# Neighbourhood attention and expert layer on one core: projections issued as late as their readers allow, a reordered opening, key loads in ScalarE's queue, image 1 loaded in pieces

## The chip, the cores and the metric

The kernel runs on one core of one Trainium2 chip. The time is the device time of one execution in microseconds. The kernel before takes 632.2 us (median of three runs, 630.95 to 632.5). The profile is of one further execution that took 633.32 us, of which 631.4 us are the recorded span.

## The reference

Two images of 48 x 48 pixels with 384 channels go through two blocks. What is computed, shortened:

```python
x = x + attention(_gn(x), registers, qkv_w, qkv_b, out_w, out_b)
x = x + experts(_gn(x), router_w, router_b, fc1_w, fc1_b, fc2_w, fc2_b)

# attention: 12 heads of 32; 16 register tokens give extra keys and values
q, k, v = split(x @ qkv_w.T + qkv_b)
k_cat, v_cat = concat(k, reg_k), concat(v, reg_v)
scores = where(mask_7x7_neighbourhood_or_register, q @ k_cat.T / sqrt(32), -1e30)
o = softmax(scores) @ v_cat
return o @ out_w.T + out_b

# experts: 4 experts with 96 hidden units each, the best 2 of a softmax router
hmid = gelu(x @ fc1.T + fc1_b) * combine
return hmid @ fc2.T + combine @ fc2_b
```

`_gn` is a group norm of 32 groups over a whole image, without weights.

## The kernel before

**Tiling.** An image has 2304 pixels: 6 tiles of 8 columns (384 pixels each, in the code `SN`) or, across them, 6 strips of 8 rows. The 12 heads are worked on in three groups of four. Image times head group makes 6 stages, and stage times tile makes 36 steps, `g` = 0 to 35. Every step has three parts, p = 0, 1, 2. Matrix products of float32 quality are made from two float16 halves: value = high + low, three products out of four.

**Units.** A unit is one projection of 384 pixels: "k" for a strip of keys (9 matmuls of 384 columns), "q" for a tile of queries (9 of the same), "v" for a tile of values (27 of 128 columns). A stage needs 18 units. TensorE computes a unit into a bank of PSUM (bank 6 in the step loop), ScalarE takes the high half out, VectorE the low half (for keys it also copies the windows into KT, `keys_low`), and a DMA writes it to DRAM: keys by SyncE (kscr), queries and values by GpSimd (qscr, vscr). They come back in another layout: KB by `keys_in` (3 DMAs a step), QS by `queries_in` (3), VR by `values_in` (6), all issued by SyncE in the kernel before. Step g's part of these is loaded one to three steps ahead.

**A part of a step.** On TensorE: scores of keys for two strips (`key_scores`, L1309), one unit of the NEXT stage (L1177), a third of the output projection of step g-2 (L1177, OS and WO), the weighted sums for two strips (`weighted`, L1328 and L1331, which need ScalarE's exponentials L984), and two groups of scores of step g+2 for the maximum (`scores`, L1279), which VectorE reduces (L609). In part 0 the maxima of step g+1 are turned (L1294), ScalarE copies them (L973) in part 1, and GpSimd sends them into two rows of QS (L413, `maxima_in`); the key scores of step g+1 wait for that DMA.

**What sets the order.** Everything is written out by hand, per engine, and bound by semaphores. In the kernel before all 18 units of stage 0 are made in the opening (six keys, then `FIRST`), and all 18 of stage n+1 within stage n by the table `NEXT`: keys in its steps 0 and 1, queries and values in steps 2 to 5. Stage 5 (steps 30 to 35) has no units; there the weighted sums lag one strip pair behind and the router's logits (L1349, L1350) stand on TensorE. The second half of the kernel, the expert layer, starts at about 484.5 us and is not touched.

**Image 1.** Its pixels are loaded by GpSimd in step 0 (L461, six DMAs of 576 KB) for the statistics and the norm; the normalised halves overwrite them in steps 6 to 11 (L914, L920, L377), and the pixels are loaded again in step 12 (L466, six DMAs of 576 KB) as the residual.

**The opening.** After the statistics of image 0, per strip: VectorE makes two float32 values (L549), ScalarE the third (L929), ScalarE three high halves (L904), VectorE three low halves (L559), then TensorE the keys of the strip.

## Time and profile before

| | |
|---|---|
| median of three runs | 632.2 us |
| profiled execution, its span | 633.32 us, 631.4 us |
| TensorE busy | 557.0 us, 88% |
| VectorE, ScalarE, GpSimd busy | 435.6, 312.5, 301.4 us |
| first key scores of step 0 (start of the step loop) | 72.40 us |
| end of step 35's last normalisation | 486.8 us |

The busy share of TensorE is high on the whole. What a change of order can win is in the stretches in which it is lower, so the windows and the chain of waits say more than the share. A step is measured below from one turn of the maxima (L1294) to the next: the turn at 75.39 us belongs to step 0, that at 91.69 us to step 1, that at 207.20 us to step 11, at 219.98 us to step 12, at 238.55 us to step 13, at 272.16 us to step 16 and at 419.10 us to step 29.

### The profile page before, as it was taken

How to read it: one execution, taken by the hardware profiler on the slowest of the kernel's cores; microseconds unless marked ns; L12 is line 12 of the kernel's file. 1: busy time of each engine (PE TensorE's matmuls, PEld its weight loads, DVE VectorE, ACT ScalarE, POOL GpSimd, SP SyncE). 2: the span in 40 equal slices, each digit the busy share in tenths (PEclk: the TensorE clock that was granted, in tenths of full speed). 3: DMA queues.
4: the chain of work that ended last, by engine and by line, in shares of the span. 5: the costliest groups of instructions: out<-in, count | busy, mean ns of one | idle time of the engine just before them, and what ended most of it. 6: DMA issues, size and time to landing. Idle time of an engine off the chain costs nothing.

```text
span 631.4 us, 22435 instructions
## 1 busy us (share of the span) xinstructions
PE 557.0 (88%) x9227; PEld 390.8 (62%) x9227; DVE 435.6 (69%) x1071; ACT 312.5 (49%) x622; POOL 301.4 (48%) x442
## 2 busy tenths in 40 slices
PE   3567969999999869999999999996988589998996
PEld 2344746767677646777677767774665346664553
DVE  6784559887976658678977898668795558763332
ACT  1762534447767624444444444556664438744321
POOL 4105746885387712556579713465554232313221
PEclk8697989999999979999999999999899799999999
DMA  9858979566866598756876588666520011211122
GB/s 309 194 140 218 277 238 219 172 174 156 198 182 167 164 320 202 206 152 182 203 186 184 156 205 210 161 175 193 128 61 6 2 38 38 77 41 54 57 76 75
DMA packets 130988, 97.79 MB, mean 155 GB/s; under 512 B 66684, under 2 KB 123944, under 8 KB 130888
## 3 DMA queue, kind: packets, MB, share of 16 engines
q1 hardware_dynamic: 120456, 73.84, 44.6%
q0 software_dynamic: 10432, 22.52, 11.5%
q8 instruction: 73, 1.20, 0.8%
q14 instruction: 27, 0.22, 0.1%
HBM read 59.83 MB, written 35.68 MB: 151 GB/s over the span
## 4 chain that ended last, share of the span: by engine, by line
PE 62%; DVE 17%; DMA 6%; issue 5%; POOL 4%; ACT 3%; SPq 2%; DVEq 0%; POOLq 0%; ACTq 0%
PE ps L1177 41%; PE ps L1309 5%; PE ps L1328 5%; PE ps L1331 4%; PE ps L1279 3%; DMA QS<-MT 3%; DVE MX L609 2%; DVE ST L511 2%; DVE KU L579 1%; DVE XH L603 1%; DMA X<-in_x 1%; DVE GT_ L549 1%; DVE KT L588 1%; PE ps L1294 1%; PE ps L1450 1%
## 5 line engine op out<-in xcount | busy, mean ns | idle before, releaser
L984 ACT ACTIVATE PT<-ps 128x448 f32<-128x448 f32 (+1 forms) x207 | 96.2, 508 | 99.0 <-PE ps L1309 98.8
L609 DVE TENSOR_REDUCE MX<-ps 128x2 f32<-128x372 f32 x216 | 106.8, 535 | 14.0 <-PE ps L1279 13.9
L1177 PE MATMUL ps<-X,WQ 128*128 128x384 f16 x486 | 89.8, 333 | 2.5 <-POOL X L377 1.6
L491 POOL TENSOR_TENSOR KT<-QS,KT 128x384 f16<-128x384 f32 x36 | 34.3, 961 | 94.6 <-ACT KT L1094 94.6
L1328 PE MATMUL ps<-PT,VR 128*32 128x112 f32 (+1 forms) x1656 | 76.6, 259 | 0.0
L1177 PE MATMUL ps<-OS,WO 128*128 128x384 f16 x324 | 70.2, 327 | 5.9 <-POOL OS L419 3.7
L1331 PE MATMUL ps<-PT,SELW 128*32 128x112 f32 (+1 forms) x1656 | 74.0, 253 | 0.0
L1177 PE MATMUL ps<-XH,WQ 128*128 128x384 f16 x324 | 62.4, 342 | 8.6 <-DVE XH L559 7.9
L1309 PE MATMUL ps<-QS,KB 122*128 122x112 f16 (+1 forms) x864 | 59.4, 213 | 11.5 <-DMA QS<-MT 11.2
L1177 PEld LDWEIGHTS ps<-X,WQ 128*128 128x128 f16 x486 | 46.1, 100 | 30.8 <-issue 4.3
L1279 PE MATMUL ps<-KB,QS 120*32 120x186 f16 x1728 | 56.8, 246 | 8.5 <-DMA QS<-qscr 5.2
L392 POOL DMA_DIRECT2D qscr<-QT x36 | 27.4, 761 | 73.4 <-DVE QT L594 70.9
L413 POOL DMA_DIRECT2D QS<-MT x72 | 37.7, 529 | 50.0 <-ACT MT L973 49.3
L1177 PE MATMUL ps<-KT,WQ 128*128 128x384 f16 x324 | 58.6, 326 | 2.9 <-DVE X L805 1.8
L1309 PEld LDWEIGHTS ps<-QS,KB 122*128 122x128 f16 x864 | 42.9, 100 | 26.4 <-issue 21.8
L1328 PEld LDWEIGHTS ps<-PT,VR 128*32 128x32 f32 x1656 | 38.8, 109 | 32.9 <-issue 29.0
L603 DVE SCALAR_TENSOR_TENSOR X<-ps,X 128x384 f32<-128x384 f32 x54 | 30.1, 557 | 39.2 <-PE ps L1177 38.7
L377 POOL TENSOR_TENSOR X<-GT_,X 128x384 f16<-128x384 f32 x36 | 35.0, 974 | 36.7 <-DVE GT_ L549 18.0
L798 DVE TENSOR_TENSOR QS<-ps,QS 128x384 f32<-128x384 f32 x36 | 19.7, 555 | 43.9 <-POOL KT L491 15.0
L1177 PEld LDWEIGHTS ps<-XH,WQ 128*128 128x128 f16 x324 | 30.8, 101 | 30.7 <-ACT XH L904 8.0
L419 POOL TENSOR_TENSOR OS<-ON,OS 128x384 f16<-128x384 f32 x36 | 32.9, 914 | 34.8 <-ACT OS L991 34.6
L1279 PEld LDWEIGHTS ps<-KB,QS 120*32 120x32 f16 x1728 | 39.3, 97 | 12.9 <-issue 7.6
(182 smaller groups left out, 1068.3 us busy)
## 6 DMA issues: line engine op xcount, KB each, us to landing
KB<-kscr SPq DMA_DIRECT2D x108, 192.0 KB, 3.8
kscr<-KT SPq DMA_DIRECT2D x36, 384.0 KB, 5.1
VR<-vscr SPq DMA_DIRECT2D x216, 56.0 KB
QS<-qscr SPq DMA_DIRECT2D x108, 96.0 KB, 3.9
...
```

What stands on the lines that cost most here:

```text
L377: nc.gpsimd.tensor_tensor(xh_block(n, blk, 1, k), tmp_block(n, k), xh_block(n, blk, 0, k), ALU.subtract).then_inc(s_["gn_lo_p"], 1)
L413: pool.dma_start(QS[SROWS + part:SROWS + part + 1, :, s * SN:(s + 1) * SN], MT[part * HEADS:(part + 1) * HEADS, g % 2, :]).then_inc(m_in[g ...
L419: nc.gpsimd.tensor_tensor(OS[:, 1, s * SN:(s + 1) * SN], ON[:, g % 2, :], OS[:, 0, s * SN:(s + 1) * SN], ALU.subtract).then_inc(s_["os_lo" ...
L491: nc.gpsimd.tensor_tensor(HW[:, m % 2, 1, k, :], HF[:, unit % 2, :], HW[:, m % 2, 0, k, :], ALU.subtract).then_inc(s_["hl"], 1)
L603: V.scalar_tensor_tensor(out=xj, in0=ps[:, op_bank(g, j), 0:SN], scalar=1 / WS, in1=xj, op0=ALU.mult, op1=ALU.add).then_inc(s_["op_done"], 1)
L609: V.tensor_reduce(out=MX[:, g % 2, t, 2 * pair:2 * pair + 2], in_=ps[:, S_BANK(i), 0:2 * RUN].rearrange("p (h n) -> p h n", h=2), op=ALU.m ...
L984: A(PTS[pt_slot(n)][:, 0:w], ps[:, ST_BANK(n), 0:w], ACT.Exp, scale=SCORE).then_inc(s_["exd"], 1)
L1177: last = mm(bank, lhsT(a, k), rhs(b, k), start=(k == 0 and n == 0), stop=(finish and k == steps - 1 and n == 2))
L1279: last = mm(ps[32 * j:32 * j + 32, S_BANK(i), hh * RUN:(hh + 1) * RUN], QS[0:SROWS, h, q0:q0 + 32], KB[0:SROWS, h, g % 4, at:at + RUN], st ...
L1309: last = mm(ps[:, ST_BANK(n), h * w:(h + 1) * w], KB[0:TROWS, h, g % 4, LEAD + CHUNK * a:LEAD + CHUNK * (a + 1)], QS[0:TROWS, h, s * SN + ...
L1328: mm(ps[DH * h:DH * (h + 1), O_BANK(g), CT_ * q0:CT_ * q1], VR[:, g % 2, a, DH * h:DH * (h + 1)], PTS[pt_slot(n)][:, h * w:(h + 1) * w], s ...
L1331: last = mm(ps[DH * h:DH * (h + 1), O_BANK(g), at:at + w], SELW[:, DH - 1 - a:2 * DH - 1 - a], PTS[pt_slot(n)][:, h * w:(h + 1) * w], star ...
```

## The change

- **Units late.** `NEXT` is replaced by `fillers(g, p)`: step g makes the values of step g+3 in part 0, the queries of step g+4 in part 1 and one key strip of the next stage in part 2, the strip (s+3) mod 6. So there are three units a step up to step 26, with one exception: the keys of stage 3 (image 1's first) are all made in steps 12 to 14, two a step, and so steps 9 to 11 have two units and steps 12 to 14 four. Steps 27 to 31 have two, step 32 one, the last three none. The lag of the weighted sums (`LAG`) begins at step 32, not 30; the router's logits and the loads and splits of the expert weights move to steps 33 and 34.
- **Opening.** 16 units instead of 18. VectorE makes all three values of a strip and the low half of the third channel block, GpSimd the low halves of the other two (`POOL_K`). The split of the first weights moves ahead of the group norm's parameters. The products of the registers and of the value bias move ahead of the first scores.
- **Key loads.** `keys_in` for steps 3 and later is issued in ScalarE's queue, between the two exponentials of part 1; in steps 3, 9, 15, 21 and 27 it first waits there until all keys of the next stage are in DRAM.
- **Image 1.** The six loads of step 0 go to steps 0 to 2, one in parts 1 and 2 each; the six of step 12 go to steps 15 to 17 in the same way.

```diff
+LAG = 32
+def fillers(g, p):
+    gi, s = divmod(g, TILES)
+    out = []
+    if p == 0:
+        out.append((gi + (s + 3) // TILES, "v", (s + 3) % TILES))
+        if gi == 2 and s < 3:
+            out.append((3, "k", 2 * s))
+    if p == 1:
+        out.append((gi + (s + 4) // TILES, "q", (s + 4) % TILES))
+    if p == 2 and gi == 2 and s < 3:
+        out.append((3, "k", 2 * s + 1))
+    elif p == 2 and (gi, s) not in ((1, 3), (1, 4), (1, 5)):
+        out.append((gi + 1 + (s + 3) // TILES, "k", (s + 3) % TILES))
+    return [u for u in out if u[0] < STAGES]
+FIRST = tuple((0, "k", i) for i in range(STRIPS)) + ((0, "q", 0), (0, "q", 1), (0, "v", 0), (0, "q", 2), (0, "v", 1), (0, "q", 3))
+BESIDE = ((0, "v", 2), (1, "k", 0), (1, "k", 1), (1, "k", 2))
-POOL_K = ((), (0, 1, 2), (0, 1, 2), ())
+POOL_K = ((0, 1), (0, 1, 2), (0, 1, 2), ())
...
 # GpSimd
-                    if g == 0:
-                        for half in range(2):
-                            at = half * 3 * SN
-                            pool.dma_start(raw1(p, at, 3 * SN), x[1, :, p, at:at + 3 * SN]).then_inc(x_in[1][p][half], 16)
-                    if g == 2 * TILES:
-                        pool.wait_ge(s_["v_mm"], 6 * KC)
...
+                    if g < KC and p:
+                        at = (p - 1) * 3 * SN
+                        pool.dma_start(raw1(g, at, 3 * SN), x[1, :, g, at:at + 3 * SN]).then_inc(x_in[1][g][p - 1], 16)
+                    if 15 <= g < 18 and p:
+                        i = 2 * (g - 15) + p - 1
...
 # VectorE, opening
             for a in range(STRIPS):
-                for k in range(2):
+                for k in range(KC):
                     normalised(0, a, k)
-                for k in range(KC):
-                    low_half(0, a, k)
+                low_half(0, a, 2)
...
 # ScalarE
+            def keys_in(g):
+                gi, s = divmod(g, TILES)
+                if s == 0:
+                    for i in range(3):
+                        act.wait_ge(kw_out[i], 32 * gi + 32)
+                if g >= 4:
+                    act.wait_ge(s_["st_mm"], 6 * (g - 3))
+                for j, part in enumerate((0, 1, 0)):
+                    nc.scalar.dma_start(KB[DH * j:DH * (j + 1), :, g % 4, LEAD:LEAD + STRIPS * CHUNK],
...
                     exps(6 * g + 2 * p)
+                    if p == 1 and g + 3 < LAST:
+                        keys_in(g + 3)
                     if gi == STAGES - 1:
                         normalised(2, s, p)
                     exps(6 * g + 2 * p + 1)
...
 # TensorE, opening
-            for a in range(STRIPS):
-                keys(0, a)
-            for kind, i in FIRST[0:6]:
-                unit(0, kind, i)
+            for u in FIRST:
+                unit(*u)
+            for g in (1, 2):
+                registers(g, 2 - g)
+            pe.wait_ge(*evicted(0, "q", 1))
+            value_bias()
             pe.wait_ge(s_["pads"], 4)
             pe.wait_ge(s_["i_in"], 16)
+            pe.wait_ge(s_["obx"], 1)
+            for p in range(3):
+                scores(0, 2 * p)
+                scores(0, 2 * p + 1)
+                unit(*BESIDE[p])
+            scores(1, 0)
+            scores(1, 1)
+            maxima_turned(0)
+            unit(*BESIDE[3])
+            for i in range(2, 6):
+                scores(1, i)
...
 # TensorE, steps
-                    if gi < STAGES - 1:
-                        unit(gi + 1, *NEXT[s][p])
+                    for u in fillers(g, p):
+                        unit(*u)
```

On TensorE the opening stood like this, from the six key strips and two query units (x72) on; x54 and x27 are value units, x9 a query unit, L1279 the scores, L1294 the turn of the maxima, the rows with RG and BVH the registers and the value bias:

```order
L1177 MATMUL ps<-XH,WQ 128x384 x72
L1177 MATMUL ps<-WQ,XH 128x128 x54
L1177 MATMUL ps<-XH,WQ 128x384 x9
L1177 MATMUL ps<-WQ,XH 128x128 x27
L1279 MATMUL ps<-KB,QS 32x186 x16
L1177 MATMUL ps<-XH,WQ 128x384 x9
L1279 MATMUL ps<-KB,QS 32x186 x16
L1177 MATMUL ps<-WQ,XH 128x128 x27
L1279 MATMUL ps<-KB,QS 32x186 x16
L1177 MATMUL ps<-XH,WQ 128x384 x9
```

And in the changed kernel, from the last query unit ahead of the registers to the first key scores of the loop (L1203 are the projections, L1311 the scores, L1324 the turn, L1339 the key scores):

```order
L1203 MATMUL ps<-RG,WQ 128x16 x9
L1203 MATMUL ps<-WQ,RG 16x128 x9
L1203 MATMUL ps<-BVH,WO 128x1 x27
L1311 MATMUL ps<-KB,QS 32x186 x16
L1203 MATMUL ps<-WQ,XH 128x128 x27
L1311 MATMUL ps<-KB,QS 32x186 x16
L1203 MATMUL ps<-XH,WQ 128x384 x9
L1311 MATMUL ps<-KB,QS 32x186 x16
L1203 MATMUL ps<-XH,WQ 128x384 x9
L1311 MATMUL ps<-KB,QS 32x186 x16
L1324 MATMUL ps<-ID,MXH 8x128 x3
L1203 MATMUL ps<-XH,WQ 128x384 x9
```

The registers now stand ahead of the first scores, where before they were behind the last; the two key units and the value unit stand between groups of scores, and there are two units fewer up to the loop.

GpSimd before, in steps 0 and 1 (L461 loads image 1, L413 sends the maxima, L430 adds the bias to image 0):

```order
L461 DMA X<-in_x 128x1152 x2
L430 ISA
L430 TENSOR_SCALAR X<-X,SM 128x384
L461 DMA X<-in_x 128x1152 x2
L413 DMA QS<-MT 1x4x384 x2
L430 TENSOR_SCALAR X<-X,SM 128x384
L461 DMA X<-in_x 128x1152 x2
L430 TENSOR_SCALAR X<-X,SM 128x384 x2
L413 DMA QS<-MT 1x4x384 x2
```

GpSimd now, in the same steps (L481 loads, L433 sends the maxima, L449 adds, L412 and L417 write queries and values to DRAM):

```order
L417 DMA vscr<-WR 16x8x128 x3
L449 TENSOR_SCALAR X<-X,SM 128x384
L433 DMA QS<-MT 1x4x384 x2
L481 DMA X<-in_x 128x1152
L412 DMA qscr<-QT 128x2x384
L449 TENSOR_SCALAR X<-X,SM 128x384
L481 DMA X<-in_x 128x1152
L449 TENSOR_SCALAR X<-X,SM 128x384
L417 DMA vscr<-WR 16x8x128 x3
L449 TENSOR_SCALAR X<-X,SM 128x384
L433 DMA QS<-MT 1x4x384 x2
L481 DMA X<-in_x 128x1152
```

Four loads stood ahead of the first maxima of the loop and six ahead of the second; now there are none and two.

ScalarE before, in one of the early steps (L984 the exponentials, L973 the copy of the maxima, L947 a key unit's high half):

```order
L984 ACTIVATE PT<-ps 128x352
L984 ACTIVATE PT<-ps 128x448
L947 ACTIVATE KU<-ps,SM 128x8x48
L973 COPY MT<-ps 8x384
L984 ACTIVATE PT<-ps 128x448 x2
L947 ACTIVATE KU<-ps,SM 128x8x48
L984 ACTIVATE PT<-ps 128x448
```

ScalarE now, in the same step (L1004 the exponentials, L992 the copy of the maxima, L986, L976 and L966 the high half of a value, a query and a key unit, L1030 the three key loads):

```order
L1004 ACTIVATE PT<-ps 128x352
L1004 ACTIVATE PT<-ps 128x448
L986 ACTIVATE WR<-ps 128x384
L992 COPY MT<-ps 8x384
L1004 ACTIVATE PT<-ps 128x448
L1030 DMA KB<-kscr 32x4x768 x3
L1004 ACTIVATE PT<-ps 128x448
L976 ACTIVATE QT<-ps,SM 128x384
L1004 ACTIVATE PT<-ps 128x448
```

The three loads stand between the two exponentials of part 1, and the copy of a unit behind them.

## Rows read from the trace of the kernel before

**Rows 1.** The page's table of busy time over the whole span.

```profile
PE 557.0 (88%) x9227; PEld 390.8 (62%) x9227; DVE 435.6 (69%) x1071; ACT 312.5 (49%) x622; POOL 301.4 (48%) x442
```

**Rows 2.** Chain that ended last: start us, length us, what was waited for.

```profile
77.84 9.26 DMA QS<-MT
...
221.74 11.35 DMA QS<-MT
```

**Rows 3.** Windows: stretch, us, busy time by engine, TensorE clock, DMA share, GB/s.

```profile
75.39:91.69 16.30, 11.05 (x210) 7.45 (x199) 8.42 (x22) 4.90 (x10) 8.02 (x10) 0.90 0.92 294
...
102.98:114.04 11.06, 11.06 (x244) 8.91 (x244) 10.18 (x25) 5.09 (x11) 9.56 (x17) 1.00 0.79 207
...
207.20:219.98 12.78, 11.15 (x238) 8.28 (x227) 8.24 (x19) 7.99 (x17) 10.64 (x18) 1.00 0.57 162
219.98:238.55 18.57, 12.90 (x218) 8.49 (x208) 9.78 (x27) 5.31 (x11) 4.02 (x7) 0.82 1.05 305
272.16:283.19 11.03, 11.03 (x255) 8.88 (x244) 7.30 (x19) 5.09 (x11) 6.25 (x11) 1.00 0.57 166
...
419.10:428.72 9.62, 9.16 (x196) 6.70 (x185) 6.70 (x15) 5.09 (x11) 5.83 (x10) 1.00 0.72 182
428.72:437.36 8.64, 7.32 (x181) 5.15 (x181) 8.05 (x24) 6.02 (x13) 4.63 (x6) 1.00 0.69 171
437.36:449.78 12.42, 8.82 (x211) 6.72 (x199) 7.30 (x17) 6.96 (x14) 4.63 (x6) 0.86 0.64 188
```

**Rows 4.** Timeline of VectorE in the opening: start us, us, line, tile, [idle].

```profile
19.52 1.35 DVE L563 SCALAR_TENSOR_TENSOR WQ<-WR,WQ 128x1152 f16<-128x1152 f32 x1
...
34.13 0.86 DVE L549 TENSOR_SCALAR GT_<-X,SM 128x384 f32<-128x384 f32 x2
...
37.46 0.86 DVE L549 TENSOR_SCALAR GT_<-X,SM 128x384 f32<-128x384 f32 x2
38.24 1.49 DVE L559 TENSOR_TENSOR XH<-GT_,XH 128x384 f16<-128x384 f32 x3
39.65 0.61 DVE L579 SCALAR_TENSOR_TENSOR KU<-ps,SM,KU 128x384 f16<-128x384 f32 x1
```

**Rows 5.** Timeline of TensorE, opening and one step.

```profile
39.88 4.55 PE L1177 MATMUL ps<-XH,WQ 128*128 128x384 f16 x27 [1.70 <-DVE XH L559]
...
53.89 0.81 PE L1279 MATMUL ps<-KB,QS 120*32 120x186 f16 x16 [3.48 <-DMA QS<-qscr]
...
72.40 0.51 PE L1309 MATMUL ps<-QS,KB 122*128 122x88 f16 x8
...
272.83 1.67 PE L1177 MATMUL ps<-WQ,X 128*128 128x128 f16 x27
...
275.33 0.37 PE L1328 MATMUL ps<-PT,VR 128*32 128x112 f32 x8
```

**Rows 6.** Timeline of GpSimd.

```profile
23.18 2.99 POOL L386 COPY KT<-KR 128x96 f16<-128x96 f16 x6 [7.83 <-DVE KR L573]
...
68.44 1.04 POOL L413 DMA_DIRECT2D QS<-MT  x2 [0.28 <-ACT MT L973]
...
72.47 1.30 POOL L386 COPY KT<-KR 128x96 f16<-128x96 f16 x6
```

**Rows 7.** GpSimd's low halves (L377): ns min/median/max, first and last start.

```profile
L377 POOL TENSOR_TENSOR X<-GT_,X x36: 906/913/2032, 155.5 to 482.1; 128x384 f16<-128x384 f32 x36
```

**Rows 8.** Timeline of ScalarE in step 16.

```profile
272.90 0.95 ACT L984 ACTIVATE PT<-ps 128x448 f32<-128x448 f32 x2
274.54 0.49 ACT L967 ACTIVATE WR<-ps 128x384 f32<-128x384 f32 x1 [0.68 <-PE ps L1177]
```

**Rows 9.** Timeline of SyncE's DMA issues, two steps.

```profile
272.75 2.64 SPq L279 DMA_DIRECT2D KB<-kscr  x3
...
407.38 1.41 SPq L279 DMA_DIRECT2D KB<-kscr  x3
```

**Rows 10.** The page's DMA issues: count, KB each, median us to landing.

```profile
kscr<-KT SPq DMA_DIRECT2D x36, 384.0 KB, 5.1
```

313 lines of the change are left out of this document (142 added, 171 removed).

## The prediction

> **What bounds the kernel now.** I read the page's busy times first: TensorE is busy for 88% of the span and no other engine for more than 69% [rows 1]. So the bound is TensorE in most stretches, and what can be won is in the others. The windows by step show which. Step 16, where nothing is in the way, takes 11.03 us with TensorE busy for all of it [rows 3]. The same work stands in steps 0, 11 and 12, which take 16.30, 12.78 and 18.57 us. The chain names the cause of two of them: 9.26 and 11.35 us of waiting for the DMA that sends the maxima [rows 2], both times just behind the loads of image 1, and in the second with the DMA engines full (share 1.05). Last I looked at the edges: the loop begins at 72.40 us [rows 5], and step 29's and 30's stretches, with a unit or more missing, still take 9.62 and 8.64 us, the next 12.42 us [rows 3]. So there are four places to price: opening, two DMA stalls, the uneven steps 9 to 14, and the end of the loop. The expert layer behind 484.5 us keeps its instructions, and I cost it at nothing.
>
> **Opening.** Before, a strip takes VectorE 37.46 - 34.13 = 3.33 us: two values 0.78, three low halves 1.41 (39.65 - 38.24), the keys' low half and windows the remaining 1.14 [rows 4]. After: three values 1.18, one low half 0.47, keys 1.14, together 2.79 us. GpSimd has two low halves, 2 x 0.91 = 1.83 us [rows 7], and for three strips two register copies, 0.43 us each alone (1.30/6 x 2) or 1.0 us beside a busy VectorE (2.99/6 x 2) [rows 6], so 2.3 to 2.8 us; ScalarE loses a value. If neither engine slows the other a strip takes 2.8 us. GpSimd's low half took up to 2.03 us instead of 0.91 [rows 7], and the register copies show the same factor beside VectorE, so I take 3.2 us; the ends are 2.8 and 4.2 (both low halves at 1.8). The split of the weights, 1.35 us [rows 4], leaves the path for the pause in which TensorE makes the group means, but the high half of the registers now stands in front of ScalarE's values, so I count 0.4 us. The last key strip begins at 39.88 us before; after at 39.88 - 0.4 - 5 x 0.13 = 38.8 us, call it X (36.7 to 43).
>
> From X on, the first scores wait for the same chain as before, key DMA out and in: 53.89 - 39.88 = 14.0 us. TensorE's six units of 1.5 us (three in 4.55 us [rows 5]) and the registers and bias (2.6 us) end at X + 13.1, so they are covered. Then come four groups of units and scores: 0.8 + 1.5 + 0.6 + 1.5 + 0.6 + 1.5 + 0.6 + turn 0.4 = 7.5 us, and the copy of the maxima and its DMA: before from 68.44 (issue) to 72.40, so 4.0 us, plus 0.6 for the copy. Loop start X + 14.0 + 7.5 + 4.6 = X + 26.1 = 64.9 us against 72.40, a gain of 7.5 us (3 to 10). About 3 us of it is two units that come back in the last steps.
>
> **Loads of image 1.** In step 0 two loads instead of six stand around the first maxima, and none directly ahead. The step then falls to what the others take: 16.30 - 11.03 = 5.3 us. GpSimd is loaded there (three additions of a bias, two loads, value and query DMAs), the maxima come later in its queue and have some 1.3 us of slack, so I give 1.0 back over steps 1 to 5: gain 4.3 (2 to 5.3). The reload goes from step 12 to steps 15 to 17: 18.57 - 11.03 = 7.5 us, and the 1.6 us by which step 11 to 12 waited for the last norm (12.78 - 11.15) is covered by the value unit that now stands ahead. I give back 0.5 for three places: gain 8.6 (6 to 9.1).
>
> A rule speaks to both. The Trainium skill, DMA: Bandwidth & Descriptors, Issuing engines are not separate DMA queues: DMAs of all issuing engines end on the same 16 engines and interleave. By it the loads cost their traffic wherever they are put, and the trace agrees so far as the share was 1.05 in step 12 [rows 3]; it says nothing against spreading them over steps with a share of 0.57.
>
> **Steps 9 to 14.** Three units of 1.5 us leave steps 9 to 11 and come into 12 to 14. In the first three ScalarE has 7.99 us of work [rows 3] plus 1.4 for the key loads, so a step can hardly fall below 10 us; I take 1.0 us gain each. In the other three each costs 1.5 us of pure TensorE time, and in part 0 the second unit needs the bank that the first has just filled: ScalarE starts the copy 0.2 us after the value unit's end (unit from 272.83 for 1.51, copy at 274.54 [rows 5, 8]) and ends 0.5 us later, so 0.7 us. Sum -3.0 + 4.5 + 2.1 = +3.6 (0 to 6).
>
> **Key loads in ScalarE's queue.** Three issues take SyncE 1.41 us, in some steps 2.64 [rows 9]. ScalarE has issued none in this trace, so the price there is bounded: from nothing (the sequencer issues while the engine calculates) to 2.64 us plus the exponential ahead. In part 1 the two exponentials begin at 272.90, 0.48 us apart, and TensorE needs the second at about 275.33 [rows 5, 8]. With 1.41 us between, it begins at 274.8 and ends at 275.3: just in time. With 2.64 it ends at 276.5, 1.2 us late. The query's copy waits behind, and with it VectorE's low half, the bank and the next key unit, which also had only tenths of slack. I take 0.1 us a step for 32 steps, +3 (0 to 12).
>
> **The last key strip.** In the third step of a stage its unit ends 1.9 us after part 2 begins; high and low half and windows follow (0.15 + 0.6 + 0.6 + 1.0 with the projection ahead of it), so the DMA leaves at 4.3 us and lands at 9.4 us with the median of 5.1 [rows 10] (the single one in the opening took about 3). ScalarE comes to its wait at 7.8 us. It would wait 1.6 us, issue 1.4, and the second exponential ends at 11.4 us; TensorE needs it at 10.2. That is 1.2 us, or nothing at 3 us of landing: 0.8 us five times, +4 (0 to 15). Behind the waiting instruction stand an exponential, a query's high half and the next step's work of ScalarE, and TensorE waits for all three. Before, SyncE held this wait, and the last strip was written in the second step of a stage, so it was hidden.
>
> **End of the loop.** Steps 27 and 28 lose a unit each, 1.3 us net of a short wait for the exponential: -2.6. The stretches from 419.10 to 484.5 us hold 65.4 us before. With five more units (7.5 us) TensorE is busy for what it idled: in the 12.42 us stretch it works 8.82, in the next 9.62 and 8.64 it works 9.16 and 7.32 while VectorE has 6.70 and 8.05 [rows 3]. I count 9.7 + 9.8 + 9.8 + 8.3 + 9.5 and 17 for the last two steps (now with the splits of the expert weights, 15.68 before) = 64.1, -1.3 (-5 to +4). Sum -3.9.
>
> **Steps 1 to 4.** VectorE has 10.18 us of work in an 11.06 us step with statistics [rows 3]; the key strip that is now in each of them adds 1.1 and takes a query of 0.5 away, so it becomes the bound there: +1.5 (0 to 3).
>
> **Sum.** -7.5 - 4.3 - 8.6 + 3.6 + 3 + 4 - 3.9 + 1.5 = -12.2 us. From 633.32 us that gives 621.1 us; the profiled run stood 1.1 us above the median of 632.2, so I forecast 620.
>
> **Rivals.**
> 1. ScalarE's waits cost, but less than is won. The last strip lands late (3 us five times, +11) and nothing else is wrong: 631, or with half of that 626. For it: 5.1 is a median among bursts, and the loads of values are in the queues at that time. Against: the key DMAs are now single.
> 2. Slower. The key loads cost ScalarE 2.6 us in every step (its own descriptor work, beside SyncE's). Place: second exponential of part 1, steps 0 to 32. Price: 1.2 us late directly and up to 0.3 through the query's copy, 1.5 x 33 = 50 less the 3 counted, +47 at full price, 667; it decides from 12.2/32 + 0.1 = 0.5 us a step, and at 0.8 a step the time is 643. For it: 1.9 to 2.6 in several steps on SyncE. Against: most are 1.4.
> 3. GpSimd and VectorE exclude each other in the opening. Strips take 4.2 us, X is 5 x 1.0 later than counted, and the opening gains 2.5 instead of 7.5: 625. For it the 2.03 us low half [rows 7] and the 2.99 us copies [rows 6]. The Trainium skill, SBUF — State Buffer, Who interferes with whom, states it as a rule: a VectorE operation with two inputs in SBUF and a GpSimd operation that reads SBUF take turns, and the later one blocks fully. The trace agrees in those two rows. Against: VectorE has one such operation a strip left where it had three.
> 4. Everything is hidden: no price at ScalarE's queue, opening at its best end: 620 - 3 - 4 - 2.5 = 610.
>
> **Numbers.** Forecast (614 to 624) 0.45, rival 1 0.18, rival 2 0.12, rival 3 0.13, rival 4 0.12. A measurement of this kernel tells 0.3%, 2 us, from no change. Of rival 1 a quarter lies within that, and a little beyond. Faster 0.82, same 0.05, slower 0.13. The range reaches down to rival 4's 607 and up to 634, past rivals 1 and 3; the forecast's own range is 614 to 624.
>
> **What would show it.** The loop starts near 65 us. No wait of TensorE for the DMA of the maxima above 2 us. Steps 12 to 14 at 13 us. ScalarE's three issues at 1.4 us, and a wait of ScalarE for the key DMA in steps 3, 9, 15, 21 and 27 of about 1.6 us, with TensorE idle ahead of L1360 in part 1 there. The step loop ends near 472 us. I am wrong if TensorE waits for exponentials in each part 1, or if VectorE and GpSimd take turns in the opening.

## The result: slower by 3.5%

The changed kernel takes 653.6 us (median of four runs, 650.2 to 658.9), the kernel before in the same session 632.0. The ratio is 1.035 with a 95% interval of 1.027 to 1.043. I had forecast 620, within 607 to 634. The profiled execution took 658.93 us with a span of 656.9 us, 5.4 us above its median; where a size matters below, medians are compared, and the profile says where. For four kernels below the median holds runs more than 1.5% above that kernel's fastest; without them it is 646.7 us instead of 649.1, 643.4 instead of 644.7, 632.7 instead of 633.1 and 630.7 instead of 636.1.

Busy time by engine, after, the page's row that answers to [rows 1]:

```profile
PE 570.0 (87%) x9227; PEld 394.8 (60%) x9227; DVE 449.5 (68%) x1065; ACT 309.8 (47%) x616; POOL 312.9 (48%) x454
```

The same 9227 matmuls take 13 us more on TensorE, and the span grows by 25.5, so the other half is idle time of TensorE. The mean granted clock was 0.953, against 0.966 before; by my estimate that makes some 8 of the 13 us (557.0 x 0.966 / 0.953 = 564.6). The chain of the first steps, after (as [rows 2]):

```profile
77.44 1.26 POOL X L449
78.70 0.53 POOL QS L433
79.23 5.20 DMA QS<-MT
...
89.12 1.25 POOL X L449
90.37 0.51 POOL QS L433
90.88 5.39 DMA QS<-MT
```

The waits of 9.26 and 11.35 us are gone. In their place stands a smaller link, again and again: GpSimd's value DMAs, in the first steps a bias addition, then the maxima, then some 5 us until they land. TensorE waited for them ten times, in the windows of steps 0 to 2, 6, 10, 11, 17, 28, 30 and 32. What TensorE waited for in the step loop, after (us in total, times, longest):

```profile
PE ps L1339 <- DMA QS<-MT: 11.3, 10, 2.4
PE ps L1324 <- DVE XH L621: 6.7, 8, 1.4
PE ps L1324 <- DVE X L621: 5.9, 6, 1.7
PE ps L1360 <- ACT PT L1004: 5.8, 11, 1.2
```

Before, the same two lines for the turn of the maxima (L1294) held 2.7 and 1.8 us in ten waits, and the maxima's DMA 11.2 us in three. So two long stalls became ten short ones, and waits for VectorE (12.6 us) and ScalarE's exponentials (5.8 us) are new. Windows by step, after, to be read against [rows 3] (same columns):

```profile
76.11:87.55 11.44, 9.79 (x228) 7.43 (x217) 6.96 (x18) 4.80 (x10) 8.27 (x12) 1.00 1.04 287
87.55:100.85 13.30, 10.46 (x231) 7.63 (x220) 9.97 (x22) 5.21 (x11) 10.76 (x15) 1.00 0.97 277
...
211.58:224.54 12.96, 11.28 (x238) 8.26 (x227) 7.92 (x19) 8.17 (x17) 9.33 (x14) 1.00 0.65 176
224.54:237.85 13.31, 12.73 (x245) 9.09 (x235) 9.28 (x25) 5.80 (x12) 4.36 (x7) 1.00 0.70 184
274.51:285.60 11.09, 11.04 (x226) 8.26 (x227) 8.02 (x21) 5.21 (x11) 5.34 (x10) 1.00 1.00 281
309.86:322.14 12.28, 11.17 (x226) 8.23 (x227) 9.95 (x24) 5.21 (x11) 8.22 (x11) 1.00 0.65 168
...
477.03:491.20 14.17, 9.76 (x228) 7.41 (x220) 9.53 (x23) 6.46 (x13) 4.58 (x6) 0.76 0.24 76
```

Step 0 fell from 16.30 to 11.44 us and step 12 from 18.57 to 13.31, as forecast; the steps beside them grew. One of the reload's steps (274.51) has TensorE busy for all of its 11.09 us with the DMA engines full (1.00), so there the load is hidden. Steps 18 to 23 are a new loss (12.28 us for step 19), and so is step 33 (14.17 us at a clock of 0.76).

The same in groups of steps, from one turn of the maxima to another in each profiled run, in us. The last two columns are two kernels of the experiments, explained there:

| steps | before | after | after, mended, keys first | before, keys first |
|---|---|---|---|---|
| first turn, at | 66.1 | 67.7 | 64.6 | 66.0 |
| 0 to 6 | 75.1 | 76.6 | 72.8 | 71.4 |
| 6 to 9 | 34.6 | 35.7 | 35.0 | 34.6 |
| 9 to 18 | 109.1 | 109.1 | 103.7 | 107.0 |
| 18 to 24 | 67.2 | 75.3 | 70.0 | 67.2 |
| 24 to 30 | 67.4 | 71.0 | 65.6 | 67.2 |
| 30 to 34 | 40.1 | 47.4 | 37.2 | 39.5 |
| last turn, at | 468.8 | 491.2 | 458.7 | 462.9 |
| span | 631.4 | 656.9 | 621.2 | 624.9 |

### The profile page after: what moved, and what is told of

It is laid out like the page before. It is cut to its first block, busy times and chain, and to the rows that moved or that the text cites. A ratio compares the mean times of both kernels' runs of the same rounds, so it can differ in the third digit from the quotient of the medians.

```text
span 656.9 us, 22437 instructions
## 1 busy us (share of the span) xinstructions
PE 570.0 (87%) x9227; PEld 394.8 (60%) x9227; DVE 449.5 (68%) x1065; ACT 309.8 (47%) x616; POOL 312.9 (48%) x454
## 3 DMA queue, kind: packets, MB, share of 16 engines
q10 hardware_dynamic: 14256, 19.47, 11.9%
## 4 chain that ended last, share of the span: by engine, by line
PE 50%; DVE 17%; DMA 11%; POOL 7%; issue 6%; ACT 5%; ACTq 2%; SPq 0%; DVEq 0%; POOLq 0%
PE ps L1203 34%; DMA QS<-MT 9%; PE ps L1339 4%; PE ps L1360 3%; PE ps L1363 2%; PE ps L1311 2%; ACTq L1030 2%; DVE ST L529 2%; DVE MX L627 2%; POOL vscr L417 2%; DVE GT_ L567 1%; DVE KU L597 1%; DVE KT L606 1%; POOL X L449 1%; DVE XH L621 1%
## 5 line engine op out<-in xcount | busy, mean ns | idle before, releaser
L1004 ACT ACTIVATE PT<-ps 128x448 f32<-128x448 f32 (+1 forms) x210 | 101.1, 512 | 120.6 <-PE ps L1339 82.9
L627 DVE TENSOR_REDUCE MX<-ps 128x2 f32<-128x372 f32 x216 | 106.5, 534 | 17.5 <-PE ps L1311 17.4
L1203 PE MATMUL ps<-X,WQ 128*128 128x384 f16 x486 | 88.9, 330 | 2.6 <-ACT WR L986 1.2
L1360 PE MATMUL ps<-PT,VR 128*32 128x112 f32 (+1 forms) x1680 | 78.4, 261 | 6.0 <-ACT PT L1004 5.8
L1203 PE MATMUL ps<-OS,WO 128*128 128x384 f16 x324 | 70.6, 328 | 6.7 <-POOL OS L439 5.1
L1203 PE MATMUL ps<-XH,WQ 128*128 128x384 f16 x324 | 67.1, 359 | 10.7 <-DVE XH L577 6.2
L1363 PE MATMUL ps<-PT,SELW 128*32 128x112 f32 (+1 forms) x1680 | 75.6, 254 | 0.0
L1339 PE MATMUL ps<-QS,KB 122*128 122x112 f16 (+1 forms) x864 | 59.7, 214 | 14.7 <-DMA QS<-MT 14.3
L1203 PEld LDWEIGHTS ps<-X,WQ 128*128 128x128 f16 x486 | 45.7, 99 | 31.1 <-issue 2.2
L1203 PE MATMUL ps<-KT,WQ 128*128 128x384 f16 x324 | 60.0, 331 | 3.2 <-DVE X L825 2.1
L412 POOL DMA_DIRECT2D qscr<-QT x36 | 27.3, 757 | 73.3 <-DVE QT L612 73.3
L1339 PEld LDWEIGHTS ps<-QS,KB 122*128 122x128 f16 x864 | 43.2, 100 | 30.4 <-issue 24.0
L1311 PE MATMUL ps<-KB,QS 120*32 120x186 f16 x1728 | 55.8, 246 | 3.2 <-DMA QS<-qscr 1.9
L621 DVE SCALAR_TENSOR_TENSOR X<-ps,X 128x384 f32<-128x384 f32 x54 | 30.1, 557 | 38.9 <-PE ps L1203 38.4
L1203 PEld LDWEIGHTS ps<-XH,WQ 128*128 128x128 f16 x324 | 32.1, 105 | 36.7 <-issue 18.3
L417 POOL DMA_DIRECT2D vscr<-WR x54 | 28.9, 540 | 46.3 <-ACT WR L986 46.2
L818 DVE TENSOR_TENSOR QS<-ps,QS 128x384 f32<-128x384 f32 x36 | 19.7, 554 | 44.8 <-POOL KT L509 15.3
L433 POOL DMA_DIRECT2D QS<-MT x72 | 38.6, 540 | 22.9 <-ACT MT L992 21.6
L621 DVE SCALAR_TENSOR_TENSOR XH<-ps,XH 128x384 f32<-128x384 f32 x54 | 29.7, 554 | 28.9 <-PE ps L1203 28.4
L1203 PEld LDWEIGHTS ps<-KT,WQ 128*128 128x128 f16 x324 | 31.2, 99 | 27.2 <-DVE X L825 3.0
```

What stands on the lines that cost most here:

```text
L412: pool.dma_start(qscr.rearrange("a p n -> p a n")[:, :, s * SN:(s + 1) * SN], QT[:, s % 2, :, :]).then_inc(q_out[s], 16)
L417: pool.dma_start(vscr[gi % 2, 16 * b:16 * b + 16, CT_ * s + 3:CT_ * s + 3 + CT_, :], VTS[s % 5][:, b, :]).then_inc(v_out[s], 16)
L433: pool.dma_start(QS[SROWS + part:SROWS + part + 1, :, s * SN:(s + 1) * SN], MT[part * HEADS:(part + 1) * HEADS, g % 2, :]).then_inc(m_in[g ...
L621: V.scalar_tensor_tensor(out=xj, in0=ps[:, op_bank(g, j), 0:SN], scalar=1 / WS, in1=xj, op0=ALU.mult, op1=ALU.add).then_inc(s_["op_done"], 1)
L627: V.tensor_reduce(out=MX[:, g % 2, t, 2 * pair:2 * pair + 2], in_=ps[:, S_BANK(i), 0:2 * RUN].rearrange("p (h n) -> p h n", h=2), op=ALU.m ...
L1004: A(PTS[pt_slot(n)][:, 0:w], ps[:, ST_BANK(n), 0:w], ACT.Exp, scale=SCORE).then_inc(s_["exd"], 1)
```

## Experiments

The theories, by the letters that the expectations use. **Q**: ScalarE's own time for issuing key loads makes its exponentials late. **G**: in GpSimd's queue the maxima stand behind value DMAs and a bias addition. **V**: VectorE and GpSimd take turns, in the opening and where window copies meet bias additions. **D**: image 1's loads cost their traffic wherever they stand. **E**: TensorE stands still at the end behind late splits of the expert weights. **M** came later: the key loads, sent from a second queue, hold up the maxima. "Before" below is the kernel before, run in the same session (631.6 to 633.1 us).

### Parts taken back, one at a time

**Key loads back in SyncE's queue**, behind the value loads of the step:

```
                 if g + 1 < LAST:
                     values_in(g + 1)
+                if g + 3 < LAST:
+                    keys_in(g + 3)        # and out of ScalarE's part 1
```

> The changed kernel with the key loads back in SyncE's queue, everything else as changed. Theory Q (ScalarE's queue is the cause): the second exponential of part 1 comes in time, the waits of TensorE for ScalarE's exponentials and the 2 to 3 us of delay in steps 3, 9, 15, 21, 27 go, 653.6 falls by 15 us or more, below 640. Theory G (in GpSimd's queue the maxima of the next step stand behind the value unit's DMAs and the bias of part 0) and theory V (VectorE and GpSimd exclude each other, in the opening and where the key windows are copied in part 2): only the delay in steps 9, 15, 21 and 27 goes, some 1.5 us each, and tenths in the others: 645 to 649.

Measured 649.1 us (ratio to before 1.025, 1.019 to 1.031), 4.5 less than after (6.9 with the median of 646.7). The maxima landed after a median of 2.0 us instead of 4.0. I read this as refuting the part of Q by which this queue is the main loss, and that was too much: in this place the keys came late themselves, and TensorE waited for them seven times, 8.1 us in all, which it had not done in the changed kernel. So the run weighs one loss against another; the kernel with the keys ahead of the values, further below, has neither.

**The maxima ahead of part 0's value DMAs and bias**, on GpSimd:

```
-                    for unit_gi, kind, i in fillers(g, p): ...; add_bias(gi // KC, p, s)
+                    for part in ((), (0, 1), (2,))[p]:
+                        for unit_gi, kind, i in fillers(g, part): ...; add_bias(gi // KC, part, s)
```

(`...` stands for `queries_out` and `values_out`, which are unchanged.)

> The changed kernel with one change of order on GpSimd: the maxima's DMA is issued ahead of the value unit's three DMAs and the bias of part 0. Theory G: the waits of TensorE for that DMA (10 of them, 11.3 us, mostly in steps 0 to 3, 6, 10 and 11, 16, 28, 31) go, the steps concerned fall from 12.5 to some 11.5 us: 10 to 15 us less, 639 to 644. Theory Q or V: the wait moves to something else that is just behind it, 650 or more.

Measured 649.6 us (1.027, 1.023 to 1.031), less than G promised. The waits for the maxima went, from 11.3 us to 1.2. Others grew: for GpSimd's low half of the output from 3.1 to 5.2 us, for the exponentials from 5.8 to 6.2, with 1.4 more ahead of the key scores.

**The opening's low halves back on VectorE:**

```
-POOL_K = ((0, 1), (0, 1, 2), (0, 1, 2), ())
+POOL_K = ((), (0, 1, 2), (0, 1, 2), ())
```

> The changed kernel with all three low halves of the opening on VectorE, none on GpSimd. Theory V: nothing takes turns then, a strip costs VectorE 1.18 + 1.41 + 1.14 = 3.7 us instead of the 4.09 us seen in the changed kernel's trace, and the loop starts 6 x 0.4 = 2 us earlier, near 71 us; total 651. If the length of a strip came from another engine (ScalarE's three high halves and key copy, 2.4 us) or from TensorE at its lower clock (3.04 us a key strip), the strip would stay at 4.09 us.

Measured 649.9 us (1.028, 1.024 to 1.033), and V is confirmed for the opening. VectorE per strip, the changed kernel (start, us), with GpSimd's two low halves of the first of these strips below it:

```profile
35.86 1.85 DVE L567 TENSOR_SCALAR GT_<-X,SM 128x384 f32<-128x384 f32 x3
37.81 1.08 DVE L577 TENSOR_TENSOR XH<-GT_,XH 128x384 f16<-128x384 f32 x1
...
39.94 1.85 DVE L567 TENSOR_SCALAR GT_<-X,SM 128x384 f32<-128x384 f32 x3
```

```profile
36.41 2.06 POOL L394 TENSOR_TENSOR XH<-GT_,XH 128x384 f16<-128x384 f32 x2 [2.03 <-DVE GT_ L567]
```

and with three low halves on VectorE instead of one:

```profile
37.90 1.25 DVE L567 TENSOR_SCALAR GT_<-X,SM 128x384 f32<-128x384 f32 x3
39.07 1.49 DVE L577 TENSOR_TENSOR XH<-GT_,XH 128x384 f16<-128x384 f32 x3
...
41.62 1.35 DVE L581 SCALAR_TENSOR_TENSOR WQ<-VR,WQ 128x1152 f16<-128x1152 f32 x1
```

A strip is 39.94 - 35.86 = 4.08 us with GpSimd's help and 41.62 - 37.90 = 3.72 without. One low half beside GpSimd takes 1.08 us (0.55 alone), three alone take 1.49. Of the three values the first two take 0.47 us each in both kernels; the third begins while GpSimd's first low half runs and takes 1.07. GpSimd itself is less slowed, 1.05 us a low half against 0.91 [rows 7]. The loop starts at 69.28 us instead of 72.94.

**The gate blocks of step 33 one step later:**

```
-{LAST - 3: (0, 1, 2), LAST - 2: (3,), LAST - 1: (4,)}
+{LAST - 2: (0, 1, 2, 3), LAST - 1: (4,)}
```

> The changed kernel with TensorE's three gate blocks of step 33 in step 34. E (TensorE stands still for 4 us behind the late split of the expert weights on VectorE and its clock falls after it): step 33 to 34 falls from 14.1 to 10 us and the loop's end comes 3 to 5 us earlier, total 648 to 651. If VectorE is what the last steps wait for in any case, the wait moves one step and the total stays at 652 to 655.

Measured 646.8 us (1.024, 1.020 to 1.029), 6.8 less than after, a little more than the 3 to 5 that E said. In the changed kernel TensorE stood still for a weight split of 0.63 us that VectorE reached late:

```profile
482.53 0.19 PE L1381 MATMUL ps<-WQ,X 128*128 128x8 f16 x1 [3.88 <-DVE WQ L587]
```

With the edit step 33 takes 9.4 us instead of 14.2. The rest of the 6.8 us is not explained, and lies within the intervals of the two medians.

### The bias additions

**Without them** (the output leaves out the bias that they add):

```
-                    if gi in (0, KC):
-                        add_bias(gi // KC, p, s)
```

> The changed kernel without GpSimd's three additions of a bias per step in the first and the fourth stage (its output leaves out that bias). V (VectorE and GpSimd take turns: the register copies of VectorE take 1.43 to 1.52 us beside a bias addition of 2.47 us, 0.58 us alone, so its projected keys are late for the turn of the maxima): steps 18 to 24, 75.3 us before the edit, fall to 69 to 71 us, and steps 0 to 6 by 2 to 4 us as well, total 642 to 647. G (the maxima stand behind value DMAs and bias in GpSimd's queue): the maxima leave 1 to 2 us earlier in these steps, and the waits of TensorE for the DMA of the maxima in steps 0 to 6 fall by half, total 644 to 648. D (the traffic of image 1's loads sets steps 0 to 2): steps 0 to 3 stay where they are and only 18 to 24 gain. If ScalarE's queue (Q) sets steps 18 to 24, they stay above 74 us.

Measured 644.7 us (1.018, 1.012 to 1.024). Steps 18 to 24 fell from 75.3 to 68.6 us, steps 0 to 6 from 76.6 to 74.7. What the additions do to VectorE shows in a key strip's two window copies. In the changed kernel:

```profile
315.08 2.47 POOL L449 TENSOR_SCALAR XH<-XH,SM 128x384 f32<-128x384 f32 x2
...
317.43 1.43 DVE L606 COPY KT<-KU 128x672 f16<-128x672 f16 x2
317.52 0.90 POOL L439 TENSOR_TENSOR OS<-ON,OS 128x384 f16<-128x384 f32 x1
```

and without the bias additions:

```profile
314.86 0.58 DVE L604 COPY KT<-KU 128x672 f16<-128x672 f16 x2
```

The copies take 2.5 times as long beside GpSimd's low half of the output. The two additions stand ahead of it in the queue and, as I read the rows, pushed it into their time. Behind them on VectorE stand the maxima and the residual (L621), for which the turn of the maxima waits.

**All three of a step in part 1, behind the maxima:**

```
+                    if gi in (0, KC) and p == 1:
+                        for c in range(KC):
+                            add_bias(gi // KC, c, s)
```

> The changed kernel with the three additions of the bias of a step moved to part 1, just behind the sending of the maxima. G: the maxima no longer stand behind a bias addition in part 0; the waits of TensorE for them in steps 0 to 6 fall by about 1 us a step, total 646 to 649. V: the same 2.5 us additions now stand beside VectorE's work of part 1 and 2, so steps 18 to 24 stay at 75 us or grow; total 650 to 655. Both can hold: then steps 0 to 6 gain and 18 to 24 don't.

Measured 643.0 us (1.017, 1.012 to 1.023): as much as leaving them out, 10.6 us, the largest single mend. Steps 0 to 6 took 73.6 us and steps 18 to 24 70.1. G holds for the first. V as I put it would have kept the second at 75; the amount of GpSimd work is the same in both kernels, so what costs is the place of the additions, what they stand beside and in front of.

### Key loads in ScalarE's queue, in the kernel before

```
-                    keys_in(g + 3)        # SyncE
+                    if p == 1 and g + 3 < LAST:
+                        keys_in(g + 3)    # ScalarE, behind the first exponential
```

> The kernel before, with only the key loads of steps 3 and later moved into ScalarE's queue, in part 1 of each step. Q as I predicted it, +3 us in all (0.1 us a step): 635. Q as the rival had it, each step 1 to 2 us longer: 660 or more. From the run with the key loads back in SyncE's queue (4 us faster than the changed kernel in the steps, steps 18 to 24 by 2.7) I expect +3 to +6 here: 635 to 638, most of it in steps with no other wait (18 to 27).

Measured 645.2 us (1.018, 1.013 to 1.024): 12 us, a third of a microsecond a step, two to four times what I expected. Little of it is waiting for ScalarE. Waits of TensorE in the loop, this kernel (before: 11.2 us in three waits for the maxima):

```profile
PE ps L1321 <- DMA QS<-MT: 18.0, 11, 6.1
PE ps L1306 <- DVE X L602: 2.1, 3, 1.2
PE ps L1340 <- ACT PT L983: 1.8, 6, 0.5
```

The exponentials cost 1.8 us, the maxima 6.8 more than before. The issues, in this kernel:

```profile
297.41 0.47 ACT L972 COPY MT<-ps 8x384 f16<-8x384 f16 x1 [1.19 <-PE ps L1306]
297.70 2.43 SPq L288 DMA_DIRECT2D QS<-qscr  x3
297.72 0.35 ACTq L1037 DMA_DIRECT2D KB<-kscr  x1
298.11 2.00 ACTq L1037 DMA_DIRECT2D KB<-kscr  x2
298.17 1.10 POOL L412 DMA_DIRECT2D QS<-MT  x2 [1.69 <-ACT MT L972]
```

and in the kernel before, where one queue sends all six loads one behind another:

```profile
294.78 1.87 SPq L279 DMA_DIRECT2D KB<-kscr  x3
295.31 1.10 POOL L413 DMA_DIRECT2D QS<-MT  x2 [1.69 <-ACT MT L973]
296.76 1.32 SPq L288 DMA_DIRECT2D QS<-qscr  x3
```

Time from issue to landing of the maxima over the loop, before and with the keys from ScalarE:

```profile
DMA to landing us min/median/max: 1.9/3.4/5.2
```

```profile
DMA to landing us min/median/max: 1.9/4.7/12.2
```

That gave theory M, and two kernels to tell it from Q.

**The same from ScalarE, in part 0** (`if p == 0 and g + 3 < LAST`):

> The kernel before with the key loads in ScalarE's queue as in the last such run (645.2 us against 633.1), but in part 0 of the step instead of part 1. There the DMA of the maxima landed after 4.7 us instead of 3.4 and TensorE waited for it 11 times instead of 3. M (new theory: the three key loads of part 1 stand in the DMA engines just ahead of the maxima, which ScalarE copies right before them, so the maxima land late): in part 0 they are through when the maxima go, landing 3 to 3.5 us, at most 4 waits, total 632 to 636. Q (ScalarE's own time for the issues): the same three issues cost the same in part 0, total 642 to 648.

Measured 635.8 us (1.007, 1.004 to 1.009), and the maxima land sooner than before:

```profile
DMA to landing us min/median/max: 1.9/2.7/4.0
```

So of the 12 us about 8 hang on the moment, and some 4 are left for ScalarE's time (TensorE waits 4.5 us for exponentials in this kernel), near the 3 that I had forecast.

**From SyncE, but not before ScalarE has copied the maxima** (`sp.wait_ge(s_["t_ev"], g + 2)` ahead of `keys_in(g + 3)`):

> The kernel before with its key loads in SyncE's queue as they were, but SyncE first waits until ScalarE has copied the maxima of part 1. M: the maxima meet the key loads as in the run from ScalarE's queue, landing 4 to 5 us, some 10 waits of TensorE for them, total 638 to 645. Q: nothing is taken from ScalarE, total 631 to 635.

Measured 633.8 us (1.004, 1.001 to 1.006), landing 3.4 us as before: M as written was wrong. The same step in this kernel:

```profile
292.92 2.16 SPq L279 DMA_DIRECT2D KB<-kscr  x3
293.19 1.09 POOL L414 DMA_DIRECT2D QS<-MT  x2 [1.69 <-ACT MT L974]
```

The key loads leave 0.27 us ahead of the maxima here, 0.45 in the kernel with ScalarE's queue and 0.53 in the kernel before. So the edit moved little in this step: already the kernel before sends its key loads at that moment, from one queue, without the loss. What differs in the kernel that takes 12 us more are the query loads. They wait behind the key loads in SyncE's queue in the kernel before and leave 1.45 us after the maxima; with the key loads gone from that queue they leave in the same microsecond. That is how I explain the 8 us. It is read from the issue times; no run holds the query loads back alone. The Trainium skill, DMA: Bandwidth & Descriptors, Queues, rings and completion order, says that a DMA engine takes packets in turn from all queues that have work. A small DMA would then be slowed by the number of queues that are full, and the landings (3.4 us with one, 4.7 with two) point that way, though no run here separates the number of queues from the number of bytes under way.

**The changed kernel, ScalarE sends in part 0** (in a stage's fourth step, where the last strip is not yet there, in part 1):

> The changed kernel with ScalarE sending the key loads in part 0 instead of part 1 (in the fourth step of a stage, where the last strip of the next stage is not yet written, still in part 1). M (the key loads leave just ahead of the maxima): the DMA of the maxima lands after 2 to 3 us instead of 4.0 to 4.2, TensorE waits for it 0 to 4 times instead of 10, the loop gets 4 to 7 us shorter, total 644 to 648. Q (ScalarE's time): exponentials are as late as before, the waits of TensorE for ScalarE stay or grow, total 650 or more.

Measured 647.2 us (1.024, 1.021 to 1.026), the maxima landing after 2.6 us, with six waits of 3.9 us in all. Total and landing are as M had them; the waits for ScalarE stayed (6.1 us), as Q says.

### Image 1's loads

**In pieces, in the kernel before** (two each in steps 0 to 2 and 12 to 14):

> The kernel before with one part of the change alone: image 1 is loaded by one DMA in parts 1 and 2 of steps 0 to 2, and again in the same way in steps 12 to 14. By the prediction's terms for the loads the two stalls go, 5.3 and 7.5 us, and about 1.5 us comes back: 632 falls to 621. Rival: the loads cost their traffic wherever they stand, and 630 or more is left.

Measured 637.2 us (1.009, 1.006 to 1.013), slower than before. Steps 0 to 3 took 9.5, 14.5, 17.8 and 12.8 us (54.5) against 16.3, 11.3, 11.1 and 11.9 (50.5); steps 12 to 16 63.0 against 63.2.

**One at a time** (`FIRST_LOADS = ((0, 1), (0, 2), (1, 1), (2, 0), (2, 2), (3, 1))`, the reload one a step in part 2 of steps 12 to 17):

> The kernel before, with image 1's first six loads spread over steps 0 to 3 and the six of the reload over steps 12 to 17, one a step in part 2. If the loads cost their traffic wherever they stand (D), 632 to 637 as with loads in pairs (637.2). If it is the pairs that fill the DMA engines ahead of a step's maxima and keys, one load of 1.5 us of all engines beside a share of 0.6 is hidden: step 12 falls from 18.6 to 11 to 12 us, steps 12 to 18 from 74.2 to 68 us, total 625 to 628.

Measured 633.1 us (1.001, 0.997 to 1.005): nothing won. Step 12 did fall to 11.0 us, and steps 13 and 14 rose to 13.0 and 14.7. In the kernel before, spreading the loads alone wins nothing; D holds there. Both runs leave the reload in steps 12 to 17; no run puts it alone into steps 15 to 17, where the changed kernel hid it (the row at 274.51 above).

### Mends together

**Four mends** (keys back on SyncE behind the values; bias behind the maxima; low halves on VectorE; gate blocks late):

> The changed kernel with four edits together: key loads back in SyncE's queue, the step's three bias additions behind the maxima in part 1, the opening's low halves on VectorE, and four of the expert layer's gate blocks one step later. If their separate gains against the changed kernel (4 to 10 us each) add up, 630 to 635; if they mend the same waits for the maxima and VectorE, 636 to 641. Under 628 only if the moved units themselves are worth what I forecast.

Measured 636.1 us (626.7 to 643.5 in four runs, too wide to say more than that it is near the kernel before). The single gains add up to 25.6 us, the four together give 17.5 (22.9 with the median of 630.7). TensorE now waited for keys, 11.4 us in six waits. The longest, and what SyncE and GpSimd sent ahead of it:

```profile
75.13 4.58 SPq L319 DMA_DIRECT2D VR<-vscr  x6
...
76.22 0.58 POOL L486 DMA_DIRECT2D X<-in_x  x1
79.76 2.31 SPq L297 DMA_DIRECT2D KB<-kscr  x3
...
88.70 0.81 PE L1305 MATMUL ps<-KB,QS 120*32 120x186 f16 x16 [5.32 <-DMA KB<-kscr]
```

**The same with image 1's loads one at a time:**

> The kernel with the four mends (636.1 us), and image 1's loads one at a time: six over steps 0 to 3, the reload one a step in part 2 of steps 15 to 20 (in it TensorE waited 11.4 us for keys, 5.3 of them behind two loads in step 1 and 4.0 in steps 17 and 18). If the pairs of loads make the keys late, these waits fall to 3 us or less and the total is 626 to 630. If the loads cost their traffic wherever they stand (D), 634 to 637.

Measured 635.2 us (1.005, 1.003 to 1.008), waits for keys 13.1 us: so the pairs of loads are not the cause.

**The same four mends, keys ahead of the values in SyncE's queue:**

```
+                if g + 3 < LAST:
+                    keys_in(g + 3)
                 if g + 1 < LAST:
                     values_in(g + 1)
-                if g + 3 < LAST:
-                    keys_in(g + 3)
```

> The kernel with the four mends, where SyncE sends a step's key loads ahead of its six value loads (some 3.4 us of issuing) instead of behind. If TensorE's 11.4 us of waiting for keys come from the place in SyncE's queue, they go and the total is 626 to 630; if from the DMA engines, which image 1's loads fill, they stay or move to the maxima and the values, 634 to 638.

Measured 625.3 us (623.1 to 627.1; ratio 0.990, 0.987 to 0.993), faster than both kernels. The key loads of the same step now leave 5.7 us earlier, no wait for them is left, and step 0 takes 9.8 us instead of 15.3. Step 1 hardly pays for it (12.9 us, 12.6 before the swap):

```profile
74.09 1.93 SPq L297 DMA_DIRECT2D KB<-kscr  x3
...
76.12 4.42 SPq L319 DMA_DIRECT2D VR<-vscr  x6
```

**All mends, but keys from ScalarE in part 0 and loads one at a time:**

> The changed kernel with all that the runs point to: ScalarE sends the keys in part 0, the bias additions stand behind the maxima, the opening's low halves are on VectorE, the gate blocks one step later, image 1's loads one at a time. If the losses of the change are these and nothing else, it beats the kernel before by its fuller last steps: 622 to 628. If units moved late have a price of their own (VectorE late for the turn of the maxima, 10 us of waits in the mended kernel), 630 to 636.

Measured 634.9 us (1.004, 1.002 to 1.007), in its second case. TensorE waited 10.0 us for exponentials, against 0.7 in the kernel just above: with the other losses gone, ScalarE's time for the issues shows.

**Keys first as the only edit to the changed kernel:**

> The changed kernel with one edit: the key loads in SyncE's queue, ahead of the step's value loads. Behind the value loads the same edit gave 649.1 us (from 653.6), in the mended kernel the turn to the front gave 10.8 us (636.1 to 625.3). If the front place is worth the same here, 637 to 641; if the maxima, which stand behind a bias addition here, then meet the key loads, 645 to 650 with landings of 3 us and more.

Measured 641.1 us (1.013, 1.009 to 1.017), at the edge of its better case: 12.5 us of the change's loss is the place of the key loads. The size is rough: two of the six runs took 635.2 us, the other four 640.7 to 641.9, and the profile is of one of the two.

**The control, keys first in the kernel before:**

> The control: the kernel before with its key loads ahead of the value loads in SyncE's queue. TensorE never waited there for keys, so if the front place only takes such waits away, 630 to 633, no change, and the 6.8 us by which the mended kernel beats the kernel before are worth of the later units. If the front place is worth 5 us or more by itself, 627 or less, and the later units bring nothing.

Measured 625.7 us (625.0 to 627.0; ratio 0.988, 0.985 to 0.992). The edit, on SyncE:

```
-                if g + 1 < LAST:
-                    values_in(g + 1)
                 if g + 3 < LAST:
                     keys_in(g + 3)
+                if g + 1 < LAST:
+                    values_in(g + 1)
+                if g + 3 < LAST:
                     queries_in(g + 3)
```

This decides what the change is worth: one swap in the kernel before gives what the changed kernel gives after four mends and a like swap. The two swaps are not quite the same, since the changed kernel's SyncE sends a step's query loads ahead of the others, and the kernel before behind the key loads. Its steps 0 and 12 (as [rows 3]):

```profile
75.91:87.30 11.39, 9.54 (x211) 6.75 (x199) 8.01 (x22) 4.89 (x10) 7.39 (x10) 1.00 1.03 356
216.67:233.90 17.23, 13.71 (x219) 8.96 (x208) 10.25 (x28) 5.31 (x11) 4.03 (x7) 0.80 1.02 314
```

Step 0 fell from 16.30 to 11.39 us without one load of image 1 being moved, and TensorE's wait for the maxima in it from 5.25 to 1.85. Over the loop the maxima land after a median of 2.6 us, not 3.4; value loads now stand between the key and the query loads. Which of the loads held the maxima up in step 0 before, the runs don't separate. Step 12 kept most of its stall (17.2 us, from 18.6).

## Why the prediction was wrong

I forecast -12.2 us and measured +21.6. Three steps of the sum carry most of the miss: 3.2 us for a strip of the opening, 0.1 us a step for the key loads, and 9.5 us for step 33. A fourth part, steps 18 to 24, had no term at all. Mechanism by mechanism:

- **Opening, -7.5: wrong, +0.5.** The loop starts at 72.94 us against 72.40. The step that failed is "so I take 3.2 us" for a strip: it took 4.08. I had allowed for GpSimd's operations to become slower beside VectorE; it was VectorE's that did, the third value (1.07 us against 0.47) and the low half (1.08 against 0.55). That was rival 3, which I gave 0.13 with the rule of the Trainium skill beside it (SBUF — State Buffer, Who interferes with whom). The low half, with two inputs, agrees with the rule: it ends 0.4 us after GpSimd's second low half does, nearly as if it had begun only then. The third value has one tensor as input, and the rule as I cited it does not speak of it. My argument against the rival, that only one two-input operation a strip is left on VectorE, overlooked it. Two rows of TensorE, changed kernel first, then the one with all low halves on VectorE, show the rest:

```profile
43.07 6.38 PE L1203 MATMUL ps<-XH,WQ 128*128 128x384 f16 x27 [1.04 <-DVE XH L577]
...
59.77 0.50 PE L1311 MATMUL ps<-KB,QS 120*32 120x186 f16 x16 [1.89 <-DMA QS<-qscr]
```

```profile
40.66 4.55 PE L1204 MATMUL ps<-XH,WQ 128*128 128x384 f16 x27 [2.09 <-issue]
...
56.09 0.81 PE L1312 MATMUL ps<-KB,QS 120*32 120x186 f16 x16 [2.46 <-DMA QS<-qscr]
```

  X was 43.1, not 38.8. From X to the first scores passed 16.7 us, not 14.0. TensorE ran at a lower clock there (three units, the last key strip the first of them, took 6.38 us and not 4.55, with a granted clock of 0.70 over them against 1.00 before), and the key and query loads took longer. Without GpSimd, and at a clock of 1.00, it is still 15.4, so even then the loop starts only 3.1 us earlier.
- **Loads of image 1, -4.3 and -8.6: the stalls went, the gain did not arrive.** Steps 0 and 12 fell as forecast (to 11.4 and 13.3 us). But steps 9 to 18, which hold the reload and the uneven units, sum to 109.1 us before and after, where I had -5.0. With the queues mended they take 103.7, the forecast to 0.4 us. The first loads' gain need not be theirs: the control gets it by the order of SyncE's queue with the loads where they were, and the pieces alone lose (637.2).
- **Key loads in ScalarE's queue, +3: the mechanism was right and not the largest one.** ScalarE's time costs about 4 us (part 0, in the kernel before). In part 1 the move costs 12. The step that failed is "I take 0.1 us a step": it priced ScalarE's time alone, and not what the maxima's DMA meets when key loads leave from a second queue beside SyncE's loads. In the kernel before those are the query loads. In the changed kernel, where SyncE sends the queries first, they are the value loads (in step 21 from 333.96 for 4.14 us, the key loads from 335.31).
- **The last key strip, +4: hardly seen.** Of the five steps only step 9 has a first key load that leaves late, 0.7 us behind the end of the exponential ahead of it. The single strips land after 3.3 us (5.1 before).
- **Steps 1 to 4, +1.5: right in kind, in the wrong place.** VectorE became late for the turn of the maxima, 12.6 us in all, but in every stage and not in steps 1 to 4 alone. I had no term for steps 18 to 24, which cost +8.1 us. There and in stage 0 the bias additions, which I mentioned only for step 0, stand in GpSimd's queue ahead of the maxima and the output's low half; moved behind the maxima they give 10.6 us back.
- **End of the loop, -3.9: wrong, some +14 by the profile (24 to 30: +3.6, 30 to 34: +7.3, last turn to the end: +3.1).** The step that failed is the 9.5 us for step 33, the last of the five stretches in my sum. I counted the splits of the expert weights in the last two steps only, but the gate blocks that the change puts into step 33 need the first split in that same step. It took 14.1 us: TensorE waited 3.88 us for the split, and the granted clock over the step was 0.76. With the gate blocks one step later it took 9.4. The 17 us for the last two steps was right (17.4 from the turn at 491.17 to the last logits), and in the mended kernel steps 29 to 33 sum to 46.8 us, where I had 47.1. Of the +3.6 in steps 24 to 30 most belongs to this one execution: in six other kernels with the same units there, these steps took 66.6 to 68.7 us.

What it adds up to: the place of the key loads 12.5 us (653.6 to 641.1), the other three mends together 15.8 (641.1 to 625.3), and what then remains of the change nothing: 625.3 against 625.7. What remains is the late units together with the new opening and image 1's loads in pieces; no run has the late units alone, so it stays open whether they win something that the other two lose. In parts they do something. The profiles of the two (table) show the mended kernel 3.3 us ahead in steps 9 to 18, 1.6 in 24 to 30 and 2.3 in 30 to 34, and behind by 1.4 in 0 to 6 and 2.8 in 18 to 24, where VectorE is still late for the turn (10.0 us of waits). Spans differ by 3.7 us, medians by 0.4, and the two were not timed in one session, so I call it no difference.

The rule of the Trainium skill that I cited for the loads (DMA: Bandwidth & Descriptors, Issuing engines are not separate DMA queues) spoke about the key loads too: it says that DMAs from several engines share the same 16 and that issuing from several saves only the issuing time. I used it for image 1 alone. That nothing was won by the second queue agrees with it; the loss of 12 us goes beyond what it says.

Rival 2, slower by ScalarE's queue, had the right sign and queue with the wrong mechanism: in the changed kernel TensorE waited for exponentials 5.8 us in all and never more than 1.2 at a time. Rival 4 comes to 610 us by its own sum, where the range names it with 607; nothing hangs on that here.

Left open: most of the profiled run's 5.4 us above the median; whether the loss from two queues at once is one of bytes or of queues; and which loads held the maxima up in the kernel before, so that the control's swap takes 5.4 us off TensorE's waits for them (11.2 to 5.8).
